# Block 0 of a convolution stack: 32-row products of four batches side by side, from shifted strip copies

## The reference

```
para = relu(conv1x1(x, pw)); para = conv3x3(para, cw)        # B, 16, H*W
xu   = patches3x3(x)                                         # B, 32*9, H*W
t    = einsum('goje,bgjp->bgoep', W, xu)                     # 32 outputs x 16 bases
out  = einsum('bgoep,bep->bgop', t, para)                    # sum over the bases
```

## Time and profile before

| what | value |
|---|---|
| runs | 383.32, 384.29, 386.93 us |
| span of the profiled execution (the page gives no time around it) | 382.3 us |
| TensorE busy / VectorE / GpSimd / ScalarE | 361.2 / 255.3 / 104.0 / 74.6 us |
| TensorE, share of the chain that ended last | 77% |
| first product of block 0 issued / last | 30.66 / 239.09 us |
| transfers, all queues | 38.32 MB |

### The profile page before, as it was taken

The page is one execution under the profiler, slowest core; times in us unless marked ns, Lnnn a source line. Parts: engine busy times, 40 slices in busy tenths (PEclk is TensorE's granted clock), DMA queues, the critical chain, the costliest instruction groups (busy, mean ns, idle before and its releaser), DMA issues.

```text
span 382.3 us, 9038 instructions
## 1 busy us (share of the span) xinstructions
PE 361.2 (94%) x3468; PEld 258.0 (67%) x3468; DVE 255.3 (67%) x447; ACT 74.6 (20%) x163; POOL 104.0 (27%) x254
## 2 busy tenths in 40 slices
PE   4899999999999999999999999999899979799993
PEld 3557888888888888888888888623266742467572
DVE  4776777977888878878878888754334176922252
ACT  1125010010100100100101000373332049552200
POOL 8527777888700000000000000133002019500001
PEclk9999999999999999999999999999999999999997
DMA  7664857617437267076273000179200000013023
GB/s 226 168 151 113 208 133 184 170 42 201 121 89 203 67 154 188 14 195 161 54 199 104 0 0 0 29 181 226 72 0 3 3 0 0 2 48 72 3 86 140
DMA packets 28833, 38.32 MB, mean 100 GB/s; under 512 B 7136, under 2 KB 23840, under 8 KB 28128
## 3 DMA queue, kind: packets, MB, share of 16 engines
q1 hardware_dynamic: 18464, 27.52, 27.9%
q10 hardware_dynamic: 10336, 10.34, 10.2%
HBM read 4.56 MB, written 2.10 MB: 17 GB/s over the span
## 4 chain that ended last, share of the span: by engine, by line
PE 77%; DVE 6%; SPq 5%; DMA 4%; ACTq 3%; ACT 2%; issue 1%; POOL 1%; POOLq 0%; DVEq 0%
PE ps L928 23%; PE ps L929 23%; PE ps L932 8%; PE ps L1104 5%; PE ps L1129 5%; SPq L372 5%; PE ps L979 3%; PE ps L1049 3%; PE ps L1073 2%; DMA X<-in_x 2%; PE ps L963 2%; ACTq L402 1%; PE ps L1089 1%; PE ps L1039 1%; ACTq L395 1%
## 5 line engine op out<-in xcount | busy, mean ns | idle before, releaser
L928 PE MATMUL ps<-WA,HS 128*128 128x512 f32 x384 | 152.7, 398 | 0.4 <-DVE HS L1193 0.4
L929 PE MATMUL ps<-WB,LS 128*128 128x512 f32 x384 | 150.5, 392 | 0.0
L1218 DVE TENSOR_TENSOR PROD<-ps,PT 128x512 f32<-128x512 f32 x128 | 88.4, 691 | 36.6 <-PE ps L932 29.7
L1202 DVE TENSOR_REDUCE RED<-PROD 128x32 f32<-128x512 f32 x128 | 86.4, 676 | 0.0
L928 PEld LDWEIGHTS ps<-WA,HS 128*128 128x128 f32 x384 | 72.1, 188 | 18.2 <-issue 0.6
L929 PEld LDWEIGHTS ps<-WB,LS 128*128 128x128 f32 x384 | 72.2, 188 | 14.4
L932 PE MATMUL ps<-WC,TS 128*128 128x512 f32 x128 | 50.1, 391 | 0.0
L762 ACT ACTIVATE HS<-HS 32x40 fp32r<-32x40 f32 x21 | 5.8, 274 | 162.4 <-DMA TS<-LO 162.0
L512 POOL MEMSET IMG<- 128x67 f32 x1 | 0.2, 155 | 136.8 <-DVE X L1208 136.8
L979 PE MATMUL ps<-SK,WE 128*32 128x512 f32 x256 | 28.2, 594 | 1.5 <-DMA SK<-IMG 1.5
L932 PEld LDWEIGHTS ps<-WC,TS 128*128 128x128 f32 x128 | 24.0, 188 | 5.0
(11 more groups left out here) (237 smaller groups left out, 343.6 us busy)
## 6 DMA issues: line engine op xcount, KB each, us to landing
LS<-HS SPq DMA_DIRECT2D x7, 960.0 KB, 5.7
HS<-HI SPq DMA_DIRECT2D x60, 80.0 KB, 2.4
SK<-IMG SPq DMA_DIRECT2D x24, 131.8 KB, 3.9
HS<-LO ACTq DMA_DIRECT2D x32, 80.0 KB, 2.7
LS<-LO ACTq DMA_DIRECT2D x32, 80.0 KB, 2.7
HS<-HI SPq DMA_DIRECT2D x30, 79.8 KB, 2.6
TS<-LO SPq DMA_DIRECT2D x34, 63.8 KB, 4.1
out_x<-OT SPq DMA_DIRECT2D x8, 256.0 KB, 2.6
```

The lines of the kernel that those rows point to most:

```text
L928: pe.matmul(ps[b][:, :], px(HS, dy), WA[:, dy, :], start=(dy == 0), stop=False)
L929: pe.matmul(ps[b][:, :], px(LS, dy), WB[:, dy, :], start=False, stop=False)
L1202: ve.tensor_reduce(RED[j % 2][:, 32 * b:32 * b + 32], PROD[b % 2][:, :].rearrange("p (o e) -> p o e", e=E0), AX.X, ALU.add).then_inc(sum_d ...
L1218: ve.tensor_tensor(PROD[b % 2][:, :].rearrange("p (o e) -> p o e", e=E0), ps[b][:, :].rearrange("p (o e) -> p o e", e=E0), para.broadcast_ ...
```

## The change

The stacks, their transfers and the zeroing of edges go. In their place ACT writes three copies of a strip of HI, one per horizontal shift (`strip_copy`, each 640 columns with the edge column left zero), GpSimd subtracts to get the same three of LO; both for two strips ahead of the block and then strip by strip, once `tile_done` says that the strip two before has been read. GpSimd's later strips stand between its other work. The weights lie as 9 taps on each batch's 32 partitions (`RA`, `WHI`, `WLO`), loaded by 12 transfers of the size of the 4 before; ACT makes the high part, VectorE the rest.

A product now takes 32 rows, the channels of one batch and one tap, so that four batches use the four row groups of the array side by side. A tile is 27 products (`PROD_TAPS`), and the four batches run 7 slots apart (`SKEW`): 3456 products in 885 slots. Tiles go through PSUM banks 0 to 5, and 6 and 7 take the sums. A pixel group's sums are turned back by four fp32 products of 32 pixels each (`back_part`), one per row group and two slots apart, each waiting until the one before is complete, since they write the same bank. The last pixel group is still turned by one transposition. VectorE sums two tiles in one instruction. Block 0 is written out, without a loop.

```diff
@@ -48,16 +48,12 @@
 EPS = 1e-5
 NT = PIX // P
 STRIP_T = 4
-SL = CR * W
...
+PLANE = (CR + 2) // 2 * W
+PROD_TAPS = 3 * TAPS
+SKEW = 7
+P_BANKS = 6
+T_SLOT = 2 * PROD_TAPS + 8
 QP = 9
-PL = (H + 2) // 2 * W
 CROWS = 8
 REP = H - CROWS + 1
 HR = CROWS + 2
...
@@ -150,18 +147,13 @@
         S3 = sb("S3", [P, 8])[0]
         top = cursor[0]
-        HI = sb("HI", [P, 2, PL + 2], F32R)[0]
...
+        HI = sb("HI", [P, 2, 3, 2, PLANE], F32R)[0]
+        LO = sb("LO", [P, 2, 3, 2, PLANE], F32R)[0]
+        RA = sb("RA", [P, TAPS, CH])[0]
+        WHI = sb("WHI", [P, TAPS, CH], F32R)[0]
+        WLO = sb("WLO", [P, TAPS, CH], F32R)[0]
...
@@ -170,7 +162,7 @@
         PO, po_at, _ = sb("PO", [P, 4 * CH])
         WR3, _, wr3_end = sb("WR3", [96, NM, 3 * C], at=po_at)
         WR3B = sb("WR3B", [96, NM, 3 * C], at=wr3_end)[0]
-        PROD = [sb(f"PROD{i}", [P, CH])[0] for i in range(2)]
+        PROD = [sb(f"PROD{i}", [P, 2 * CH])[0] for i in range(2)]
         RED = [sb(f"RED{i}", [P, P])[0] for i in range(2)]
         assert cursor[0] <= nc.sbuf_usable_end, (cursor[0], nc.sbuf_usable_end)
...
@@ -378,44 +365,24 @@
         def copy_bank(i, b):
             return ps[COPY_BANKS[4 * i + b]]
-        def plane_rows(m, k, t):
...
+        def strip_rows(s, dx):
+            c0 = max(dx - 1, 0)
+            c1 = W + min(dx - 1, 0)
+            a = s * CR * W
+            return UB[:, a:a + 2 * PLANE].rearrange("p (r t c) -> p t r c", t=2, c=W)[:, :, :, c0:c1]
+        def strip_copy(m, s, dx):
+            c0 = max(1 - dx, 0)
+            c1 = W + min(1 - dx, 0)
+            return m[:, s % 2, dx, :, :].rearrange("p t (r c) -> p t r c", c=W)[:, :, :, c0:c1]
+        def strip_pixels(m, b, g, tap):
+            t = g % STRIP_T
+            r = t // 2 * 4 + t % 2 + tap // 3
+            return m[32 * b:32 * b + 32, g // STRIP_T % 2, tap % 3, r % 2, r // 2 * W:r // 2 * W + P]
         def load_x(queue, k):
...
@@ -437,38 +404,15 @@
             for p, i, h, dy in ((low, 0, 0, 0), (high, 0, 0, 1), (high, 0, 1, 0), (low, 1, 0, 2), (low, 1, 1, 1), (high, 1, 1, 2)):
                 sp.dma_start(CWB[p, 3 * i:3 * i + 3, E0 * h:E0 * h + E0], cw[:, dy, :, :]).then_inc(w_cw, 16)
-            for g in range(3):
...
+            for i in range(3):
+                for b in range(B):
+                    sp.dma_start(RA[32 * b:32 * b + 32, 3 * i:3 * i + 3, :], w0[3 * i:3 * i + 3, :, :].rearrange("t c n -> c t n")).then_inc(w_main[i], 16)
             sp.wait_ge(pt_done, 4)
             sp.dma_start(WR3[:, :, :], w3a).then_inc(w_l3, 16)
             sp.dma_start(WR3B[:, :, :], w3b).then_inc(w_l3, 16)
             for g in range(4):
                 sp.dma_start(W1R[32 * g:32 * g + 32, :, :], w1).then_inc(w_l1, 16)
-            sp.wait_ge(hi_done, 2 * NCH)
-            sp.wait_ge(lo_done, 2 * NCH)
...
@@ -542,23 +484,14 @@
                 gp.tensor_copy(CWB[32 * g:32 * g + 32, :, :], CWB[0:32, :, :]).then_inc(cw_copied, 1)
                 gp.wait_ge(cw_copied, g)
             gp.wait_ge(norm0_done, NCH)
-            def lo(n):
...
+            def lo(s):
+                for dx in range(3):
+                    gp.wait_ge(hi_done, 3 * s + dx + 1)
+                    gp.tensor_tensor(strip_copy(LO, s, dx), strip_rows(s, dx), strip_copy(HI, s, dx).bitcast(F32), ALU.subtract).then_inc(lo_done, 1)
+            lo(0)
+            lo(1)
             step(gp.memset(AVG[:, :, :], 0.0))
             for b in range(B):
...
@@ -617,6 +550,7 @@
                 step(gp.tensor_scalar(cy, cy, 0.0, None, ALU.max))
                 step(gp.tensor_tensor(cy, cy, CX[:, :], ALU.mult))
+            lo(2)
             gp.wait_ge(w_l1, 64)
             for y in range(4):
                 step(gp.tensor_tensor(WT[:, :, :], W1R[:, :, :], CO[:, y:y + 1, :].broadcast_to([P, C, TAPS]), ALU.mult))
...
@@ -632,6 +567,7 @@
                 for e in range(1, NM):
                     step(gp.tensor_scalar(raw[:, e, :], raw[:, e, :], PAR[0:96, AL + e:AL + e + 1], None, ALU.mult))
                     step(gp.tensor_tensor(eff, eff, raw[:, e, :], ALU.add))
+            lo(4)
             step(gp.memset(EMASK[:, :], 0.0))
             for e in range(NE):
                 step(gp.memset(EMASK[32 * e:32 * e + 32, e:e + 1], 1.0))
@@ -648,6 +584,8 @@
             step(gp.tensor_scalar(SDIAG[:, :], AVG[:, 0, :], S3[:, 0:1], None, ALU.mult))
             step(gp.tensor_scalar(SDIAG2[:, :], AVG[:, 0, :], S3[:, 2:3], None, ALU.mult))
             gp.memset(CT[:, :], 0.0).then_inc(mix_ready, 1)
+            for s in range(5, NCH):
+                lo(s)
             gp.wait_ge(tile_done, B * NT)
             gp.wait_ge(x1_done, NCH)
             clear_border(IMG)
...
@@ -720,17 +658,23 @@
             for k in range(1, NCH, 2):
                 load_x(act, k)
             act.wait_ge(zeroed, Z_BORDER)
-            def hi(n):
...
+            def hi(s):
+                if s >= 2:
+                    act.wait_ge(tile_done, B * STRIP_T * (s - 1))
+                act.wait_ge(norm0_done, min(s + 2, NCH))
+                for dx in range(3):
+                    act.activation(strip_copy(HI, s, dx), strip_rows(s, dx), ACT.Copy).then_inc(hi_done, 1)
+            def weights_hi(i):
+                act.wait_ge(w_main[i], 64)
+                act.activation(WHI[:, 3 * i:3 * i + 3, :], RA[:, 3 * i:3 * i + 3, :], ACT.Copy).then_inc(w0_hi, 1)
             act.activation(SROW[:, 0:1], MHALF[:, 0:1], ACT.Relu)
-            for n in range(3):
...
+            hi(0)
+            hi(1)
+            weights_hi(0)
             act.wait_ge(w_par, 16)
             act.wait_ge(rstd_ready, 1)
             act.wait_ge(pw_edge_done, 1)
@@ -741,8 +685,8 @@
...
-            act.wait_ge(lo_done, 3)
-            stack_lo(act, 0, 0, first_lo)
+            weights_hi(1)
+            weights_hi(2)
             for j in (0, 2):
                 act.wait_ge(para_conv_done, j + 1)
                 act.activation(PO[:, j * CH:(j + 1) * CH], ps[j][:, :], ACT.Identity, bias=PAR[:, CB:CB + 1]).then_inc(para_by_scalar, 1)
@@ -750,28 +694,8 @@
...
@@ -915,62 +839,74 @@
                     ins = pe.transpose(ps[4 + j][:, u * P:(u + 1) * P], PO[:, a:a + P], ID[:, :])
                 ins.then_inc(pt_done, 1)
-            def tile(half, t, b, third_late=False):
+            def product_tap(g, b, i):
+                n, tap = B * g + b, i % TAPS
+                if i == 0 and n >= P_BANKS:
+                    pe.wait_ge(product_done, n - P_BANKS + 1)
+                elif i == 0 and n == 4:
+                    pe.wait_ge(pt_by_vector, 1)
+                elif i == 0 and n == 5:
+                    pe.wait_ge(pt_by_scalar, 1)
+                if b == 0 and g % STRIP_T == 0 and i == 0:
+                    pe.wait_ge(hi_done, 3 * (g // STRIP_T + 1))
+                elif b == 0 and g % STRIP_T == 0 and i == TAPS:
+                    pe.wait_ge(lo_done, 3 * (g // STRIP_T + 1))
+                if n == 0 and i < TAPS and i % 3 == 0:
+                    pe.wait_ge(w0_hi, i // 3 + 1)
+                elif n == 0 and i >= 2 * TAPS and i % 3 == 0:
+                    pe.wait_ge(w0_lo, tap // 3 + 1)
+                m, wt = ((HI, WHI), (LO, WHI), (HI, WLO))[i // TAPS]
+                ins = pe.matmul(ps[n % P_BANKS][:, :], strip_pixels(m, b, g, tap), wt[32 * b:32 * b + 32, tap, :],
+                                start=(i == 0), stop=(i == PROD_TAPS - 1))
+                if i == PROD_TAPS - 1:
+                    ins.then_inc(tile_done, 1)
+            def sums_rows(g):
+                t = g % STRIP_T
                 r = t // 2 * 4 + t % 2
...
+                return sums_bank(g // STRIP_T % 2).rearrange("p (r c) -> p r c", c=W)[:, r:r + 3:2, :]
+            def back_part(g, part):
+                if part == 0:
+                    pe.wait_ge(sum_done, 2 * g + 2)
+                    if g % STRIP_T == 0 and g >= 2 * STRIP_T:
+                        pe.wait_ge(x1_done, g // STRIP_T - 1)
+                else:
+                    pe.wait_ge(part_transposed, 3 * g + part)
+                p = slice(32 * part, 32 * part + 32)
+                ins = pe.matmul(sums_rows(g)[:, part // 2, part % 2 * 32:part % 2 * 32 + 32], RED[g % 2][p, :], ID[p, p], start=True, stop=True)
+                ins.then_inc(sums_transposed if part == 3 else part_transposed, 1)
+            def back(g):
+                pe.wait_ge(sum_done, 2 * g + 2)
+                pe.transpose(sums_rows(g), RED[g % 2][:, :], ID[:, :]).then_inc(sums_transposed, 1)
+            def block0():
+                for slot in range(PROD_TAPS * NT + SKEW * (B - 1)):
                     for b in range(B):
-                        if not (first and j == 0):
...
+                        g, s = divmod(slot - 2 * b - T_SLOT, PROD_TAPS)
+                        if s == 0 and 0 <= g < NT - 1:
+                            back_part(g, b)
+                        g, i = divmod(slot - SKEW * b, PROD_TAPS)
+                        if 0 <= g < NT:
```

(56 more changed lines are left out.)

214 lines of the change are left out of this document (23 added, 191 removed).

## The result

| | before | changed kernel |
|---|---|---|
| median of the runs on the same chip | 384.12 us | 392.94 us (390.21 to 394.77) |
| span of the profiled execution | 382.3 us | 392.3 us (its run took 394.12) |
| first / last product of block 0, recorded starts | 30.66 / 238.93 us | 30.68 / 246.27 us |
| last addition to X, and from there to the end of the span | 241.77, 140.5 us | 250.19, 142.1 us |
| all transfers | 38.32 MB | 14.24 MB |

The changed kernel takes 1.0214 times as long, 95% interval 1.0153 to 1.0275: it is slower, by about 2% (the interval leaves open on which side of 2%). 385.1 us was forecast, and 392.94 lies within the range of 375.0 to 398.5.

A forecast was written before the change was run, and what follows sets the result against it. Block 0 was taken to run at the pace of TensorE's product stream. Terms -2.5 - 3.4 + 6.8 + 0.4 - 0.5 = +0.8 us on the median of 384.29 gave 385.1 us, no change; range 375 to 398.5 us.

The forecast's parts named there:

- case D: Block 0: the stage starts late or the part waits don't fit, +2 to +8 us, 387 to 393 us; chance 0.08.
- rival B: Block 0: a small part holds up all row groups, products starting in program order; +13.3 us, 398.4 us; chance 0.16.
- product stream: Block 0 on TensorE: 885 slots against 896 products, a slot at a product's 0.2293 us; -2.5 us.
- 31 transpositions gone: Block 0 on TensorE: 31 transpositions of sums leave the stream, 0.11 us of uncovered weight load each; -3.4 us.
- the parts' own price: Block 0: each part costs only its row group two 0.11 us loads, 0.22 us per pixel group; +6.8 us, bounds 3.4 to 27.3.
- the new wait: Block 0: each part waits for the one before, complete after 0.43 us against two slots, 0.46; +0.4 us, bounds 0 and 10.
- start: Ahead of block 0: preparation hidden, first product moves from 30.74 to about 30.2 us; -0.5 us, bounds -0.7 and +1.5.
- end of the block: Tail of block 0: one reduction over two tiles stands where 1.28 us for two reductions stood; 0 us.
- work after the block: Code behind block 0: given no term in the forecast's sum; 0 us.
- rival A: Block 0, faster: fp32r product overhead shrinks, slot 0.2217 us, -6.7 us, 378.4 us; at the floor 0.2133, 371; chance 0.22.
- C: Block 0, slower: four fp32r streams are too much for a port, 0.283 us a slot, +47 us, 432 us; chance 0.06.

The follow-up runs named there:

- no parts: Changed kernel without the 124 small products that turn the sums back, nothing waiting for them, sums not added: 378.43 us, ratio to before 0.9794.
- part 0 alone: Changed kernel with only the first of the four small fp32 products per pixel group, the other three and their waits left out: 383.35 us, single run.
- 3 slots: Changed kernel with its four fp32 parts 3 slots apart instead of 2: 387.12 us, ratio to before 1.0008.

## Why the prediction was right and wrong

The time lay in the range, but the likeliest case, no change, didn't happen. What happened is the second half of case D (the part waits don't fit, up to 393 us), which I gave 0.08. That the range held it is in part luck: its upper end came from rival B, which is refuted.

| step | on record, us | measured, us | from |
|---|---|---|---|
| product stream | -2.5 | 885 x 0.2267 - 896 x 0.2293 = -4.8 | no parts |
| 31 transpositions gone | -3.4 | not measured by itself | |
| the parts' own price | +6.8 | 31 x 0.27 = +8.4 | part 0 alone, 3 slots |
| the new wait | +0.4 | 31 x (6.61 - 6.39) = +6.8 | 2 slots against 3 |
| start | -0.5 | 0 | 30.68 against 30.66 us |
| end of the block | 0 | 3.92 - 2.84 = +1.1 | clock at 0.50 |
| work after the block | 0 | 142.1 - 140.5 = +1.6 | see below |

The sum is 9.7 us, the two spans differ by 10.0. These are two single executions; the medians differ by 8.8 us. The first four rows, the block itself, give 7.0, where the traces have 215.6 - 208.3 = 7.3, and the rest goes with stretches at the lower clock, as shown below.

- **The product stream** was right in its kind. Four row groups side by side run at the full array's pace, 0.2267 us a slot against the 0.2293 that I took from before. That 0.2293 is an average: in the trace of before the products start 0.225 to 0.236 us apart, most often 0.227, and the slots just don't have the longer distances. The 0.2217 of rival A isn't reached, and C falls with its 0.283. By the Trainium skill's 3.07 (TensorE: Matmul & The Clock Gate, Part 3, "Measured speedup vs the span model") I had estimated 0.299 us a slot; the trace doesn't agree, with 0.2267 in the kernel without parts.
- **The parts' own price** was right in its mechanism: 0.22 forecast, 0.27 measured, whether one row group has a part or all four. The kernel with 3 slots has a block of 209.1 us (30.73 to 239.79), where I forecast 209.5 (my own terms add up to 208.9 + 1.3 = 210.2). That it fits so well is luck: cheaper slots and a dearer part cancel. B, that all row groups pay for each part, would have given 4 x 0.22 less one slot; it is refuted. I had named for it the strict order of starts and ends that the Trainium skill states (TensorE: Matmul & The Clock Gate, Part 3, "The mechanism"); as a price for each part the traces don't bear it out, 0.27 us for one part and for four.
- **The new wait is the step that failed.** I put a part's completion at 0.43 us after it begins, against two slots, 0.46, called that a fit and took 0.4 us; it cost 6.8. The trace records when the completion is signalled (medians over the pixel groups): 0.63 us after part 0 begins, 0.44 after part 1, 0.63 after part 2. Each waiting part's load starts 0.04 us behind that signal, so all three waits hold their part up. Two things were wrong, then. The completion of parts 0 and 2 is 0.2 us later than I put it. And the next part doesn't need it when its product starts but when its load could go ahead, 0.22 us earlier: part 1 completes as I had it, and part 2's load, at 105.20, is still only 0.11 us ahead of its product. Where the load isn't ahead, it lies open, with the loads of all row groups behind it. The bound of 10 us held it, the value taken didn't.
- **Why completion varies** isn't shown. A part that is the only one of its pixel group signals 0.31 us after it begins; with parts 3 or 4 slots apart it is 0.31 to 0.33 us for part 0 and 0.55 to 0.71 for the others (medians). At 3 slots parts 2 and 3 still follow their signal by 0.04 us (medians), with their loads 0.11 us ahead and not 0.22, and yet the period is that of one part alone. So not every late signal costs time, and how 0.8 us of lateness over the four parts becomes 0.22 us of period I can't work out.
- **The start.** ScalarE was in time, as worked out. VectorE was not: 1.76 us for a subtraction was read where GpSimd was on other work, and I moved GpSimd's reads of SBUF beside it, at 2.93 us on average. Moving them away gave 1.0 us.
- **The end.** The clock fell in the drain of the row groups in three of the thirteen executions of the new layout that were profiled, and VectorE's last addition was then 3.9 to 4.1 us behind the last product instead of 2.8. In the other ten it stayed at 1.00 there, so the 1.1 us are not a fixed cost of the layout. That the fall belongs to the drain is read from the windows of the three, not shown by an experiment.
- **After the block** the same code took 139.3 to 145.0 us in the thirteen traces, 139.3 to 140.4 where the mean granted clock was 0.996 or more and 142.7 to 145.0 where it was 0.984 or less. The clock records say where it comes from. With no stretch at 0.50 between the block and the last few us it took 139.3 to 140.4 us (three traces; before, 140.5), with one of 3.4 us 141.3 to 142.1 (three, the changed kernel among them), with two 142.7 to 143.5 (five), with three 145.0, with a single one of 10.2 us 143.5. So a stretch costs 1 to 2 us, and the 1.6 us of the table are the one stretch that the trace of before doesn't have. Nothing shows that the change brings it: the mean clock of the changed kernel's four executions was 0.983 to 0.996, and executions of the kernel before have 0.977 to 0.998.

Open is why a part's own price is 0.27 and not 0.22. What the removed transpositions cost no run isolates. The trace of before supports the 0.11: from a transposition at 102.29 to the second product behind it at 102.63 it is 0.34 us, and a product is 0.227 of that.

## What to carry to other kernels

A wait between two TensorE instructions should be over when the weight load of the second could go ahead, one product before it starts: count from load to load, and take the completion from its signal in the trace rather than from the product's duration (here 0.3 to 0.7 us after the start). A part that waits holds back the loads of all row groups behind it. Small fp32 products that only move data are better written as transpositions, in one pass (0.15 us a pixel group for 0.27). Four in four row groups cost no more than one, while one over the full array cost 0.52 us. Before a wait is given more room, follow who waits for its end: with one slot too many here VectorE was late, and gave it back to TensorE.

## What the hardware showed beside this

- Four fp32r products of 32 rows and 512 columns, one in each row group, take 0.2267 us together, and the last six products of the block, which one row group has to itself, start 0.227 us apart too.
- VectorE's subtraction with two inputs in SBUF (1536 columns): 1.72 us by itself, 3.11 where GpSimd's (640 columns) ran beside it throughout; GpSimd's goes from 1.56 to 3.07 us.
- The completion of one and the same small fp32 product was signalled between 0.31 and 0.7 us after its start (medians by place), depending on where it stood; why isn't shown.
- A transposition over 128 rows between row groups that run apart: 0.52 us.
- The granted clock can fall to 1.2 GHz although TensorE has a product under way at every moment: it did so in three of thirteen traces, at 0.50 for 3.4 us, after a stretch in which first three, then two, then one of the four row groups had products.
